# FiLM moved to tokens on partitions in both layers of a two-layer conditioned transformer block: a DMA transposes its output, ScalarE and GpSimd share the normalizations, ScalarE masks V

## The chip, the cores and the metric

The kernel runs on one core of one Trainium2 chip. The metric is device time in microseconds of one execution; the lower the better. The number to beat is the median of three runs of the kernel before, 825.99 us (822.73 to 827.06).

## The reference, cut to what matters

Two layers run one after the other on `x` of shape (32, 256, 256): 32 independent batches of 256 tokens with 256 features. Layer 0 is linear attention with 8 heads (softmax of Q over a head's 32 features, of K over the tokens), layer 1 is full attention with 16 heads of 16 features. Both end in the same way, and the change is about this ending and about the layer norms.

```python
# layer 0 (x: b, t, d)
xn = ln(x) * ln_w + ln_b
q = softmax(heads(xn @ Wq + bq), axis=-1)
k = softmax(heads(xn @ Wk + bk + (1 - mask) * -1e6), axis=tokens)
v = heads((xn @ Wv + bv) * mask)
y = q @ (k.T @ v)
# layer 1
xn = ln(x) * norm_w + norm_b
att = softmax(q @ k.T + (1 - mask) * -1e6, axis=keys)
v = (xn @ v_w + v_b) * mask
y = att @ v
# the ending of each layer ("FiLM")
scale, shift = split(silu(cond) @ W_emb + b_emb)          # per batch, 256 features each
h = ln(y) * ln2_w + ln2_b
h = silu(h * (1 + scale) + shift) @ W_out + b_out
x = x + h
```

So in the ending a row of `A` and a row of `B` per batch (both 256 long, made once in the setup from scale, shift, ln2_w and ln2_b) are applied to the normalized `y`, silu follows, and a matmul with `W_out`.

## The kernel before, in words

A batch is two blocks of 128 tokens on the partitions, 256 features along the free dimension ([128, 2, 256], 512 fp32 values in each partition). The kernel streams the 32 batches through some 60 small pieces; each piece is one to eight instructions on one engine, and has a semaphore that counts batches. The order of the pieces is written out by hand in one list for each engine (the lists of calls such as `rows(12, 3); cols(11, 4); ...`), so every engine works in a fixed order and waits for the semaphores of the piece that is next. Layer 0 runs several batches ahead of layer 1, so that in most of the program all engines hold work of both layers. PSUM has 8 banks; tables (`BANK`, `FREED`) say which bank a piece writes for each batch and what has to be finished before. All DMAs are issued by SyncE ("SPq" in the profile), also from one written list.

Pieces that the change touches, each with a suffix 0 or 1 for the layer:

- Norm of x (`a`, `n`, `r`, `c`, `h`, `z`): VectorE aggregates mean and variance (L1207), ScalarE writes minus the mean (`nm`, L1681) and variance plus epsilon (`ve`, L1682), GpSimd takes the power -1/2 (`rs`, L2011), GpSimd writes the normalized `Z` (two instructions of 256, L2015), GpSimd rounds it to fp16 (`h`, L2029), GpSimd subtracts for the remainder (`z`, L2036). The fp16 pair `ZHL` is transposed by a DMA (L531) and feeds the matmuls; each projection is three fp16 products (high x high, low x high, high x low), 12 matmuls in all.
- Norm of y (`yn`, L2015 with `YN`), by GpSimd, with tokens on partitions.
- FiLM: TensorE transposes `YN` (`y0T`, `y1T`: four 128x128 fp32 transposes in a bank, L723). With features on partitions, `A` and `B` of a batch are one number in each partition, so ScalarE applies them as scale and bias of an activation straight from PSUM: `TH` = tanh(h/2) (L1758) and `HH` = h (L1761), two instructions of 256 each. VectorE makes `ST` = (TH + 1) * HH (L1278). ScalarE rounds it to fp16 (`SH`, L1771), GpSimd subtracts for the remainder (L2088), and the output projection reads the pair (L708 with `wo`).
- Mask of V in layer 1 (`vm`, L2129): GpSimd, two instructions of 256.

The other large consumers are the scores of layer 1, computed twice: as rows (L835, with VectorE's maximum L1308 behind it, 8 pieces of four matmuls in a batch) and as columns (L848, with ScalarE's exponential L1807 behind it), then the product with V (L861).

Of the kernel before, what the change touches and what calls it, by code (L numbers as in the profile page):

```python
# [29 lines left out]
    "gpm": "1",  # L30
    "gt_w0": "0",
    "grow3": "2",
    "ga_w0": "0",
    "gt_o0": "3",
    "gcnd": "4",
    "gbb0": "5",
    "ga_o0": "3",
    "gbb1": "0",
    "gk0": "24753705446136211562401264736663",
    "gq0": "42207151427077545476112375444722",  # L40
    "gfx0": "6",
    "gv0": "75642771253063150447530557625531",
    "gkt": "66726405663127011101160224236724",
    "gfm0": "3",
    "gat": "65212575415247151554334140721664",
    "gqt": "73355127624732065226236537346625",
    "gt_f0": "3",
    "gy0": "25750625603626114224256013761365",
    "ga_f0": "4",
    "gy0T": "42355207464664435223011576172432",  # L50
    "gt_w1": "1",
    "ga_w1": "1",
    "go0": "05413576502340043030735727070451",
    "grw": "6",
    "gcol": "6",
    "gt_b": "4",
    "gt_o1": "0",
    "ga_b": "4",
    "gfx1": "1",
    "gq1": "44704575141572521727150770612041",  # L60
    "ga_o1": "0",
    "gk1": "75525464633014417236046551205400",
    "gfm1": "3",
    "gt_f1": "4",
    "gbb2": "2",
    "gv1": "64057773630271362144236527064014",
    "gr0": "00402404646460424404200042262666",
    "gr1": "62206262662206620026644420602242",
    "gr2": "20622202222220660020444444260466",
    "gr3": "62624600022200624246404264020442",  # L70
    "gr4": "02664642426266600642200260006626",
    "gr5": "26022200042600006026040424264222",
    "gr6": "62204402044006044042460246206600",
    "gr7": "26640640022262066220206664662262",
    "ga_f1": "6",
    "gc0": "66426404266406666262424400644262",
    "gc1": "20002246622242422000020042264004",
    "gc2": "60042246260062646020604422046660",
    "gc3": "62422004646244460644620060624202",
    "gc4": "46206646662204044604426046062024",  # L80
    "gpv0": "14062153063330626002061215650456",
    "gc5": "66404004646604464266226402462060",
    "gpv1": "15143460474541250413602344706447",
    "gpv2": "45043560446454250516700255304554",
    "gc6": "20606626000222626620064660624002",
    "gc7": "00224244662606662264242026460020",
    "gty0": "46056577455433510066701742216543",
    "gpv3": "31754730007352047562301275105572",
    "gty1": "33267244665003044624440055105472",
    "gy1T": "71477300023554175724706543174653",  # L90
    "go1": "77002057550012516235333440150322",
# [189 lines left out]
def up(n):  # L281
    return max(n, 0)


def bass_cond_seq(
# [7 lines left out]
    with ctx:  # L293
# [407 lines left out]
        def _(e):  # L701
# [318 lines left out]
            def fm0():  # L1020
                film(0)
# [1244 lines left out]
```

## Time and profile before

| | before |
|---|---|
| median of 3 runs | 825.99 us |
| the profiled execution | 826.59 us |
| its span (first to last instruction) | 824.9 us |
| PE busy | 797.7 us (97%) |
| DVE busy | 735.6 us (89%) |
| ACT busy | 704.5 us (85%) |
| POOL busy | 688.7 us (83%) |
| granted TensorE clock | 0.989 |

PE is TensorE, PEld its weight loads (they run beside the matmuls), DVE is VectorE, ACT ScalarE, POOL GpSimd, SPq the queue of SyncE that issues DMAs. Busy is the time in which at least one instruction of the engine runs. Instructions of one engine overlap at their ends: the next one starts before the last has ended. So what an instruction costs in an engine that is never idle is the distance from its start to the next start, which is less than its duration. A timeline row merges neighbours of one kind: start, length of the merged stretch, what, and how many.

### The profile page before, as it was taken

How to read it: one execution, taken by the hardware profiler on the slowest of the kernel's cores; microseconds unless marked ns; L12 is line 12 of the kernel's file. 1: busy time of each engine (PE TensorE's matmuls, PEld its weight loads, DVE VectorE, ACT ScalarE, POOL GpSimd, SP SyncE). 2: the span in 40 equal slices, each digit the busy share in tenths (PEclk: the TensorE clock that was granted, in tenths of full speed). 3: DMA queues.
4: the chain of work that ended last, by engine and by line, in shares of the span. 5: the costliest groups of instructions: out<-in, count | busy, mean ns of one | idle time of the engine just before them, and what ended most of it. 6: DMA issues, size and time to landing. Idle time of an engine off the chain costs nothing.

```text
span 824.9 us, 27262 instructions
## 1 busy us (share of the span) xinstructions
PE 797.7 (97%) x9407; PEld 572.0 (69%) x9407; DVE 735.6 (89%) x1488; ACT 704.5 (85%) x1658; POOL 688.7 (83%) x1021
## 2 busy tenths in 40 slices
PE   7998999999999999999999999999999999999995
PEld 3575776777777777677777777777777777666643
DVE  6899999998989999989898889989898989898962
ACT  2366678999898998898898998889989999999995
POOL 8579899999878999789898999888889987896423
PEclk9899999999999999999999999999999999999998
DMA  7522355354344443334545543353454433444411
GB/s 184 153 40 67 96 140 133 81 119 112 86 108 109 105 126 102 98 90 98 122 107 136 121 98 84 84 134 106 110 122 109 109 88 80 99 104 128 116 34 39
DMA packets 149276, 86.11 MB, mean 104 GB/s; under 512 B 87404, under 2 KB 141802, under 8 KB 149130
## 3 DMA queue, kind: packets, MB, share of 16 engines
q1 hardware_dynamic: 149140, 84.36, 42.4%
q8 instruction: 77, 1.26, 0.7%
q14 instruction: 59, 0.48, 0.2%
HBM read 39.64 MB, written 25.80 MB: 79 GB/s over the span
## 4 chain that ended last, share of the span: by engine, by line
PE 41%; issue 12%; POOL 9%; DVE 9%; DMA 2%; SPq 1%; ACT 1%; POOLq 0%; DVEq 0%; ACTq 0%
PE banks L708 11%; PE banks L861 7%; PE banks L716 5%; PE banks L835 4%; PE banks L848 4%; PE banks L723 3%; DVE NM L1308 3%; PE banks L738 2%; PE banks L787 2%; PE banks L871 2%; DVE st L1199 1%; POOL YN L2015 1%; POOL rs L2011 1%; POOL ZHL L2036 1%; POOL SH L2088 1%
## 5 line engine op out<-in xcount | busy, mean ns | idle before, releaser
L1308 DVE TENSOR_REDUCE NM<-banks 128x4 f32<-128x1024 f32 x256 | 306.4, 1212 | 25.1 <-PE banks L835 24.0
L1807 ACT ACTIVATE wraw<-banks 128x1024 f32<-128x1024 f32 x154 | 155.9, 1034 | 8.0 <-PE banks L848 7.3
L2011 POOL TENSOR_TENSOR rs<-ve,nhalf 128x2 f32<-128x2 f32 x128 | 89.7, 703 | 31.6 <-ACT ve L1682 31.4
L1807 ACT ACTIVATE PX<-banks 128x1024 f32<-128x1024 f32 x102 | 103.5, 1035 | 8.6 <-PE banks L848 7.3
L2088 POOL TENSOR_TENSOR SH<-ST,SH 128x512 f16<-128x512 f32 x64 | 74.4, 1164 | 31.4 <-ACT SH L1771 31.4
L708 PE MATMUL banks<-wo,SH 128*128 128x256 f16 x768 | 94.9, 274 | 4.5 <-POOL SH L2088 4.4
L708 PE MATMUL banks<-wv,ZT 128*128 128x256 f16 x768 | 93.5, 273 | 1.4 <-DVE wv L1404 0.5
L835 PE MATMUL banks<-SK,SQ 51*128 51x256 f16 x1024 | 92.5, 272 | 0.8 <-ACT wemb L1815 0.3
L848 PE MATMUL banks<-SQ,SK 53*128 53x256 f16 x1024 | 90.6, 271 | 2.1 <-DVE NM L1308 1.0
L2036 POOL TENSOR_TENSOR ZHL<-Z,ZHL 128x256 f16<-128x256 f32 x128 | 87.5, 704 | 2.6
L861 PE MATMUL banks<-wraw,V 128*32 128x256 f32 x1232 | 87.2, 385 | 0.8 <-DVE NM L1308 0.8
L708 PEld LDWEIGHTS banks<-wo,SH 128*128 128x128 f16 x768 | 72.1, 98 | 20.7 <-POOL SH L2088 7.1
L708 PEld LDWEIGHTS banks<-wv,ZT 128*128 128x128 f16 x768 | 73.0, 98 | 15.3 <-issue 7.3
L2115 POOL TENSOR_TENSOR AB<-R,AB 128x512 f16<-128x512 f32 x64 | 74.6, 1168 | 3.8 <-ACT AB L1787 3.5
L2015 POOL TENSOR_SCALAR Z<-X,nm,rs 128x256 f32<-128x256 f32 x128 | 73.9, 586 | 4.2 <-issue 2.5
L1787 ACT ACTIVATE R<-banks,fcs 128x256 f32<-128x256 f32 x128 | 62.3, 487 | 12.3 <-PE banks L716 12.0
L1758 ACT ACTIVATE TH<-banks,hB,hA 128x256 f32<-128x256 f32 x128 | 65.8, 571 | 7.6 <-PE banks L723 6.9
L2015 POOL TENSOR_SCALAR YN<-Y,nm,rs 128x256 f32<-128x256 f32 x128 | 70.1, 557 | 1.3
L848 PEld LDWEIGHTS banks<-SQ,SK 53*128 53x128 f16 x1024 | 39.9, 94 | 41.7 <-issue 24.0
L1761 ACT ACTIVATE HH<-banks,fB,fA 128x256 f32<-128x256 f32 x128 | 66.2, 581 | 0.0
L835 PEld LDWEIGHTS banks<-SK,SQ 51*128 51x128 f16 x1024 | 38.8, 94 | 36.8 <-issue 23.0
L1787 ACT ACTIVATE AB<-banks,fcs 128x256 f16<-128x256 f32 x128 | 62.8, 491 | 0.0
(186 smaller groups left out, 1879.5 us busy)
## 6 DMA issues: line engine op xcount, KB each, us to landing
scr<-AB SPq DMA_DIRECT2D x64, 256.0 KB, 2.6
X<-in_x_dram SPq DMA_DIRECT2D x32, 256.0 KB, 2.8
SK<-scr SPq DMA_DIRECT2D x64, 128.0 KB, 2.9
SQ<-scr SPq DMA_DIRECT2D x64, 128.0 KB, 2.7
out_dram<-wemb SPq DMA_DIRECT2D x32, 256.0 KB, 2.5
SK<-scr SPq DMA_DIRECT2D x64, 64.0 KB, 2.9
SQ<-scr SPq DMA_DIRECT2D x64, 64.0 KB, 2.7
wemb<-in_L_cond_W_emb_dram SPq DMA_DIRECT2D x1, 1024.0 KB, 5.5
```

What stands on the lines that cost most here:

```text
L708: m = PE.matmul(dst[:, t, :], zt[:, j, k, t * P:(t + 1) * P], w[:, i, k, :], start=(k, n) == (0, 0), stop=(k, n) == (1, 2))
L835: m = PE.matmul(banks[:, n + j % 2, (j // 2) * T:(j // 2) * T + T], SQ[p, r, h, c * P:(c + 1) * P], SK[p, r, h, :], start=True, stop=True)
L848: m = PE.matmul(banks[:, n + j % 2, (j // 2) * T:(j // 2) * T + T], SK[p, r, h, c * P:(c + 1) * P], SQ[p, r, h, :], start=True, stop=True)
L861: m = PE.matmul(banks[32 * j:32 * j + 32, n, 0:T], V1[:, r, c, 4 * g + j, :], px((8 * b + u) % 5)[:, at_px(j):at_px(j) + T], start=(c == 0 ...
L1308: V.tensor_reduce(NMe[:, c, :, 2 * g:2 * g + 2], banks[:, n:n + 2, :].rearrange("p a (h m) -> p a h m", m=T), AX.X, ALU.max, negate=True). ...
L1787: t = A.activation(dst, bank(home(f"g{c}1", b))[:, f, :], ACT.Identity, bias=fcs[:, i, f:f + 1], scale=(r_q, r_k)[i])
L1807: A.activation(px(v % 5), banks[:, n:n + 2, :].rearrange("p a n -> p (a n)"), ACT.Exp, scale=r_uu).then_inc(S["exp"])
L2011: G.tensor_tensor(rs[:, b % 2, l, :], ve[:, b % 2, l, :], nhalf[:, :], ALU.pow).then_inc(S[f"r{l}"])
L2015: i = G.tensor_scalar(dst[:, t, :], src[:, t, :], nm[:, b % 2, l, t:t + 1], rs[:, b % 2, l, t:t + 1], ALU.add, ALU.mult)
L2036: i = G.tensor_tensor(ZHL[:, l, b % 2, 1, k], z[:, :, k, :], ZHL[:, l, b % 2, 0, k], ALU.subtract)
L2088: G.tensor_tensor(SH[:, l, 1], ST[:, l], SH[:, l, 0], ALU.subtract).then_inc(S[f"sl{l}"])
L2115: G.tensor_tensor(AB[:, i, :, 1], R1[:, i], AB[:, i, :, 0], ALU.subtract).then_inc(S["sp" + c])
```

## The change

FiLM is done with tokens on partitions. The row `A` and the row `B` of a batch (`FR`, [128, 2, 256]) are spread to all partitions by a DMA for each batch and layer (`fr0`, `fr1`) from a table in DRAM that is written once (`fw0`, `fw1`). The normalized y goes straight to `HH`; GpSimd multiplies it by `A` (`fa`) and adds `B` (`fb`), 512 wide each; ScalarE takes the tanh of `HH`, in one instruction of 512 from SBUF (`th`); `ST` is as before; `SHL` is its fp16 pair with the remainder in two halves; a DMA transposes it (`sT0`, `sT1`, [128, 1024] fp16) into `SHT`, which the output projection reads. TensorE's transposes `y0T` and `y1T`, and their banks, are gone.

Three smaller parts: the rounding to fp16 in the norms of x (`h0`, `h1`), the normalized x of layer 0 (`c0`), the normalized y of layer 0 (`yn0`) and the mask of V (`vm`) go from GpSimd to ScalarE; where ScalarE normalizes, VectorE makes -mean*rs first (`m0`, `my0`); where GpSimd does (`c1`, `yn1`), it subtracts the mean that VectorE aggregated, so that ScalarE's `nm` is gone. In the setup, VectorE prepares the rows with batches on 32 partitions (`film_token`). All lists of order and the bank tables are written anew.

```diff
             def o0(b):
-                e.wait_ge(S["sl0"], b + 1)
+                e.wait_ge(d_s[0][b % 2], 16 * (b // 2 + 1))
...
-            def y0T(b):
-                e.wait_ge(S["yn0"], b + 1)
-                clear(e, "gy0T", b)
-                transposes(home("gy0T", b), YN[:, 0]).then_inc(S["y0T"])
...
+            def film_in(b, l, i):
+                e.wait_ge(S[f"fb{l}"], b)
+                if b == 0:
+                    e.wait_ge(l_fm[l], 16)
+                e.dma_start(FR[:, i].rearrange("p a n -> p (a n)"), fmd[l, b].unsqueeze(0).to_broadcast([P, 2 * D])).then_inc(d_fr[l][b % 2], 16)
+
+            def turn_out(b, l, i):
+                e.wait_ge(S[f"sl{l}"], b + 1)
+                e.wait_ge(S[f"o{l}"], b)
+                e.dma_start(SHT[:, i].rearrange("p j k (t n) -> p (j k t) n", t=2),
+                            SHL[:, i].rearrange("p j k t n -> p (j k t n)"), transpose=True).then_inc(d_s[l][b % 2], 16)
...
+            def m0(b):
+                e.wait_ge(S["r0"], b + 1)
+                e.wait_ge(S["c0"], up(b - 1))
+                for t in range(2):
+                    i = V.tensor_scalar(nmr[:, b % 2, 0, t:t + 1], mv[:, b % 2, 0, t, 0:1], rs[:, b % 2, 0, t:t + 1], -1.0,
+                                        ALU.mult, ALU.mult)
+                i.then_inc(S["m0"])
...
-                A.activation(nm[:, b % 2, l, :], mv[:, b % 2, l, :, 0], ACT.Copy, scale=-1.0)
...
-                for k in range(2):
-                    A.activation(TH[:, l, k, :], bank(n)[:, k, :], ACT.Tanh, bias=hB[:, l, k, b:b + 1],
-                                 scale=hA[:, l, k, b:b + 1])
-                for k in range(2):
-                    i = A.activation(HH[:, l, k, :], bank(n)[:, k, :], ACT.Identity, bias=fB[:, l, k, b:b + 1],
-                                     scale=fA[:, l, k, b:b + 1])
+                e.wait_ge(S["fb0"], b + 1)
+                e.wait_ge(S["st0"], b)
+                A.activation(TH[:, 0], HH[:, 0], ACT.Tanh, scale=r_t[0]).then_inc(S["th0"])
...
+            def h0(b):
+                e.wait_ge(S["c0"], b + 1)
+                if b >= 2:
+                    e.wait_ge(d_z[0][b % 2], 16 * (b // 2))
+                A.activation(ZHL[:, 0, b % 2, 0].rearrange("p k t n -> p t k n"),
+                             Z[:, 0].rearrange("p t (k n) -> p t k n", k=2), ACT.Identity).then_inc(S["h0"])
...
+            def c0(b):
+                e.wait_ge(S["m0"], b + 1)
+                e.wait_ge(S["z0"], b)
+                for t in range(2):
+                    i = A.activation(Z[:, 0, t, :], X[:, b % 3][:, t, :], ACT.Identity, bias=nmr[:, b % 2, 0, t:t + 1],
+                                     scale=rs[:, b % 2, 0, t:t + 1])
+                i.then_inc(S["c0"])
...
+            def fa0(b):
+                e.wait_ge(S["yn0"], b + 1)
+                e.wait_ge(d_fr[0][b % 2], 16 * (b // 2 + 1))
+                G.tensor_tensor(HH[:, 0], HH[:, 0], both(FR[:, 0, 0, :]), ALU.mult).then_inc(S["fa0"])
+
+            def fb0(b):
+                e.wait_ge(S["fa0"], b + 1)
+                G.tensor_tensor(HH[:, 0], HH[:, 0], both(FR[:, 0, 1, :]), ALU.add).then_inc(S["fb0"])
```

What the change does to ScalarE's order is shown at one place in the middle of the program. Before, from the start of `th1` of some batch (`banks` is PSUM, `wemb` here the buffer of the transposed attention output, `PX` and `wraw` the buffers of exponentials):

```order
L1807 ACTIVATE PX<-banks 128x1024
L1815 ACTIVATE wemb<-banks 128x256
L1807 ACTIVATE wraw<-banks 128x1024
L1758 ACTIVATE TH<-banks,hB,hA 128x256 x2
L1761 ACTIVATE HH<-banks,fB,fA 128x256 x2
L1736 ACTIVATE AT<-banks 32x2x32 x4
```

ScalarE after, near the same place, with `yn0` (L1933), `c0` (L1925), `h0` (L1911) and `th0` (L1788):

```order
L1933 ACTIVATE HH<-Y,nmr,rs 128x256 x2
L1828 ACTIVATE wraw<-banks 128x1024
L1730 ACTIVATE KE,ks<-banks,km 128x256 x2
L1708 ACTIVATE ve<-mv,epa 128x2
L1925 ACTIVATE Z<-X,nmr,rs 128x256 x2
L1911 ACTIVATE ZHL<-Z 128x2x2x128
L1788 ACTIVATE TH<-HH 128x512
L1753 ACTIVATE QT<-banks,rk 128x256 x2
```

The four instructions of FiLM from PSUM became one from SBUF, and `h0` stands straight behind the `c0` whose result it reads.

SyncE's queue, also in the middle. Before, the DMA transposes there are of `ZT` (layer inputs) and `NT` (row maxima):

```order
L588 DMA_TRANSPOSE NT<-NMw 128x2x128
L524 DMA X<-in_x_dram 128x2x256
L595 DMA ntd<-NT 32x256
L531 DMA_TRANSPOSE ZT<-ZHL 128x8x128
L551 DMA scr<-AB 128x4x256
L602 DMA SQ<-ntd 2x2048 x2
```

SyncE after, with the transposes of FiLM's output (L522) and the rows `FR` (L517):

```order
L522 DMA_TRANSPOSE SHT<-SHL 128x8x128
L560 DMA_TRANSPOSE ZT<-ZHL 128x8x128
L617 DMA_TRANSPOSE NT<-NMw 128x2x128
L522 DMA_TRANSPOSE SHT<-SHL 128x8x128
L573 DMA augm<-mbd 3x256
L517 DMA FR<-fmd 128x512
L624 DMA ntd<-NT 32x256
```

In each batch two transposes and two spreading DMAs are new, and `ZT` and `NT` stand among them in one queue.

## Rows read from the trace of the kernel before

**Rows 1.** The page's first part: busy time of each engine over the span.
```profile
PE 797.7 (97%) x9407; PEld 572.0 (69%) x9407; DVE 735.6 (89%) x1488; ACT 704.5 (85%) x1658; POOL 688.7 (83%) x1021
```
**Rows 2.** Windows of the span: each engine's busy time, clock, DMA share.
```profile
0.00:100.00 100.00, 89.58 (x735) 60.96 (x737) 88.17 (x249) 52.90 (x157) 78.75 (x129) 0.93 0.45 106
100.00:700.00 600.00, 594.34 (x7327) 441.82 (x7330) 550.41 (x1074) 541.15 (x1289) 536.22 (x789) 1.00 0.45 108
700.00:800.00 100.00, 98.80 (x1204) 61.50 (x1198) 88.76 (x148) 95.34 (x187) 65.48 (x95) 1.00 0.38 99
800.00:825.00 25.00, 14.97 (x152) 7.72 (x148) 8.23 (x21) 15.14 (x29) 8.23 (x10) 0.91 0.13 43
```
**Rows 3.** The same window for L1308 alone, eight in a batch.
```profile
100.00:700.00 600.00, 246.73 (x207) 1.00 0.45 108
```
**Rows 4.** Timeline of PE at 407 us: two neighbouring groups of four transposes.
```profile
407.67 0.60 PE L723 MATMUL banks<-ident,KE 128*128 128x128 f32 x4
408.10 0.60 PE L723 MATMUL banks<-ident,QE 128*128 128x128 f32 x4
```
**Rows 5.** Timeline of ACT from 399 us: start, stretch, what.
```profile
399.45 0.68 ACT L1720 ACTIVATE QE<-QS 128x512 f32<-128x512 f32 x1
399.97 0.25 ACT L1681 ACTIVATE nm<-mv 128x2 f32<-128x2 f32 x1
400.06 0.34 ACT L1682 ACTIVATE ve<-mv,epa 128x2 f32<-128x2 f32 x1
...
403.54 0.47 ACT L1704 ACTIVATE KE<-banks,km 128x256 f32<-128x256 f32 x1
403.90 0.20 ACT L1704 ACTIVATION_READ_ACCUMULATOR KE<-banks,km 128x1 f32 x1
...
418.91 1.02 ACT L1758 ACTIVATE TH<-banks,hB,hA 128x256 f32<-128x256 f32 x2
419.82 1.02 ACT L1761 ACTIVATE HH<-banks,fB,fA 128x256 f32<-128x256 f32 x2
```
**Rows 6.** Timeline of POOL from 419 us: `c0` and `vm`.
```profile
419.63 1.10 POOL L2015 TENSOR_SCALAR Z<-X,nm,rs 128x256 f32<-128x256 f32 x2
...
429.02 0.93 POOL L2129 TENSOR_SCALAR V<-V1t,mcol 128x256 f32<-128x256 f32 x2
```
**Rows 7.** Groups of POOL's lines: busy us, mean ns of one | idle before.
```profile
L2036 POOL TENSOR_TENSOR ZHL<-Z,ZHL 128x256 f16<-128x256 f32 x128 | 87.5, 704 | 2.6
L2088 POOL TENSOR_TENSOR SH<-ST,SH 128x512 f16<-128x512 f32 x64 | 74.4, 1164 | 31.4 <-ACT SH L1771 31.4
L2029 POOL TENSOR_SCALAR ZHL<-Z 128x256 f16<-128x256 f32 x128 | 54.5, 441 | 2.9
L2071 POOL TENSOR_TENSOR XB<-X,bobc 128x512 f32<-128x512 f32 x32 | 40.7, 1273 | 4.6 <-DVE X L1289 4.5
```
**Rows 8.** Timeline of DVE at 410 us: a pair of tiny instructions, the next one.
```profile
410.79 0.25 DVE L1207 BATCH_NORM_AGGREGATE mv<-st 128x2 f32<-128x6 f32 x2
410.97 0.75 DVE L1289 SCALAR_TENSOR_TENSOR X<-banks,un,XB 128x512 f32<-128x512 f32 x1
```
**Rows 9.** L1278 alone: count, duration ns min/median/max.
```profile
L1278 DVE SCALAR_TENSOR_TENSOR ST<-TH,HH x64: 629/693/1678, 49.9 to 816.9; 128x512 f32<-128x512 f32 x64
```
**Rows 10.** L1278 as a group: busy us, mean ns | idle before.
```profile
L1278 DVE SCALAR_TENSOR_TENSOR ST<-TH,HH 128x512 f32<-128x512 f32 x64 | 51.9, 816 | 4.0 <-ACT HH L1761 4.0
```
**Rows 11.** L531 alone: SyncE's time for one (min/median/max ns), and its landing.
```profile
L531 SPq DMA_TRANSPOSE ZT<-ZHL x64: 1231/1241/2533, 14.5 to 762.4; - x64
...
DMA to landing us min/median/max: 3.0/3.2/5.6
```
**Rows 12.** Waits of SyncE's queue, the largest: us in total, times, longest.
```profile
SPq L588 <- DVE NMw L1313: 114.6, 28, 7.5
```
**Rows 13.** Timeline at 813 us: the last batch's `yn1` and `st1`.
```profile
813.13 1.09 POOL L2015 TENSOR_SCALAR YN<-Y,nm,rs 128x256 f32<-128x256 f32 x2
...
816.94 0.69 DVE L1278 SCALAR_TENSOR_TENSOR ST<-TH,HH 128x512 f32<-128x512 f32 x1 [3.63 <-ACT HH L1761]
```

More of the change, by code:

```diff
@@ L275 @@
 PIECES = (
-    "s0 a0 n0 r0 c0 h0 z0 xb0 k0 km kn ke ktT kt rk q0 q1 qm qs qe qtT qt qd rq v0 v att at y0 Y0 s1 a1 n1 r1 "
-    "yn0 y0T th0 st0 sh0 sl0 o0 x1 s2 a2 n2 r2 c1 h1 z1 xb1 q1p qa spq k1p ka spk v1p vt vm rows max nh np cols "
-    "exp pv yt ty rd Y1 s3 a3 n3 r3 yn1 y1T th1 st1 sh1 sl1 o1 o").split()
+    "s0 a0 n0 r0 m0 c0 h0 z0 xb0 k0 km kn ke ktT kt rk q0 q1 qm qs qe qtT qt qd rq v0 v att at y0 Y0 s1 a1 n1 r1 "
+    "my0 yn0 fa0 fb0 th0 st0 sh0 sl0 o0 x1 s2 a2 n2 r2 c1 h1 z1 xb1 q1p qa spq k1p ka spk v1p vt vm rows max nh np cols "
+    "exp pv yt ty rd Y1 s3 a3 n3 r3 yn1 fa1 fb1 th1 st1 sh1 sl1 o1 o").split()
 def up(n):
@@ L408, in bass_cond_seq @@
         ST = sb("ST", [P, 2, 2, T])
-        SH = sb("SH", [P, 2, 2, 2, T], F16)
+        FR = sb("FR", [P, 2, 2, D])
+        SHL = sb("SHL", [P, 2, 2, 2, 2, P], F16)
+        SHT = sb("SHT", [P, 2, 2, 2, T], F16)
+        tsc = sb("tsc", [P, 2])
         AB = sb("AB", [P, 2, 2, 2, T], F16)
@@ new lines, in _ @@
+            x_in(24); wq(18); rk6(18); rq6(18); fr1(15); sT1(14); z1T(19); sT0(20); nT(17); am(26); nw(17)
+            out_(14); z0T(24); nr(17); fr1(16); x_in(25); wk(19); fr0(22); wq(19); rk6(19); rq6(19); sT1(15)
+            z1T(20); nT(18); sT0(21); out_(15); nw(18); z0T(25); x_in(26); fr0(23); fr1(17); wk(20); nr(18); wq(20)
+            rk6(20); am(27); z1T(21); rq6(20); sT1(16); nT(19); sT0(22); nw(19); nr(19); z0T(26); fr0(24); wk(21)
+            x_in(27); wq(21); rk6(21); am(28); rq6(21); sT1(17); z1T(22); fr1(18); sT0(23); nT(20); nw(20)
@@ L1204, in moments @@
                 e.wait_ge(S[f"s{l}"], b + 1)
-                e.wait_ge(S[f"n{l}"], up(b - 1))
+                e.wait_ge(S[("c0", "yn0", "c1", "yn1")[l]], up(b - 1))
                 for t in range(2):
@@ L1674, in _, with spread @@
             r_un, r_q, r_k, r_uu = (e.alloc_register(n) for n in ("r_un", "r_q", "r_k", "r_uu"))
-            def mean_of(b, l):
+            r_t = [e.alloc_register(f"r_t{l}") for l in range(2)]
+            def spread(b, l):
                 k, a = l % 2, (ZS ** -2, 1.0)[l % 2]
@@ L2137, in yn1, with fa1, fb1 @@
                 e.wait_ge(S["r3"], b + 1)
-                e.wait_ge(S["y1T"], b)
-                apply(b, 3, YN[:, 1], Y[:, 1], "yn1")
-            def sl1(b):
-                sl_of(b, 1)
+                e.wait_ge(S["st1"], b)
+                apply(b, 3, HH[:, 1], Y[:, 1], "yn1")
+            def fa1(b):
+                e.wait_ge(S["yn1"], b + 1)
+                e.wait_ge(d_fr[1][b % 2], 16 * (b // 2 + 1))
+                G.tensor_tensor(HH[:, 1], HH[:, 1], both(FR[:, 1, 0, :]), ALU.mult).then_inc(S["fa1"])
+            def fb1(b):
+                e.wait_ge(S["fa1"], b + 1)
+                G.tensor_tensor(HH[:, 1], HH[:, 1], both(FR[:, 1, 1, :]), ALU.add).then_inc(S["fb1"])
+            def sl1(b):
+                e.wait_ge(S["sh1"], b + 1)
+                for k in range(2):
+                    i = G.tensor_tensor(SHL[:, 1, 1, k], ST[:, 1].rearrange("p t (k n) -> p t k n", k=2)[:, :, k, :],
+                                        SHL[:, 1, 0, k], ALU.subtract)
+                i.then_inc(S["sl1"])
             def cst():
```

1283 lines of the change are left out of this document (647 added, 636 removed), and 178 rows, old and new, of the table FREED.

## The prediction, made before the changed kernel was run

> **What bounds the kernel now.** I read the busy times of the page first [rows 1]: TensorE is at 97% and the others at 83 to 89%. The windows say where the missing 27 us of TensorE are [rows 2]: 10.4 in the first 100 us (setup and the first batches), 5.7 in the 600 us between 100 and 700, 1.2 in the next 100, 9.9 in the last 25. So from 100 to 800 us TensorE is the bound: it works 99% of the time at the full clock (1.00, the 2.4 GHz level), while VectorE idles 50 us of the 600, ScalarE 59, GpSimd 64. Those idle times are waits on a saturated TensorE and on each other, and they are the slack that an edit of these engines can use. The window of L1308 shows 207 of eight in a batch [rows 3], so the 600 us hold about 25.8 batches, 23.3 us each; TensorE's share of that is 23.0.
>
> **What an instruction costs.** With engines this full the distance of starts counts, not the duration. Four fp32 transposes take 0.43 us from start to start [rows 4]. On ScalarE, 512 values from SBUF without operands in SBUF take 0.52 (399.45 to 399.97), a tiny one 0.09, 256 values from PSUM with one operand per partition 0.36, with two 0.455 (two in 0.91) [rows 5].
>
> **The change part by part, per batch.**
>
> TensorE loses two groups of four transposes. 0.43 each where they stand beside their like; groups that begin behind a wait cost a little more, so I take 0.45: -0.90 us, 23.3 over the middle's 25.8 batches and 29 over 32. The output projections stay 12 matmuls. The setup loses eight small transposes, under 1 us.
>
> ScalarE loses eight activations of 256 from PSUM with two operands (8 x 0.455 = 3.64) and four `nm` (0.36): -4.0. It gains two `th` and two `h` of 512 from SBUF (4 x 0.52 = 2.08), four of 256 with two operands for `c0` and `yn0`, and two with one for `vm` (0.72). `c0` and `yn0` read SBUF with two operands per partition, for which the trace has no row; the nearest rows are 0.36 and 0.52, and I take the two-operand row, 0.455: 1.82. Sum +4.62, net +0.62. In its order `h0` stands straight behind the `c0` that it reads, which loses the overlap of neighbours, about 0.1. I take +0.7: ScalarE's 541 us of the middle become 559. (The Trainium skill, "ScalarE: Activation LUTs", section "What ACT_TABLE_LOAD costs", gives for an activation 186 ns + 0.833 per value, 93 per pointer operand, and an overlap of 93: an estimate of 0.49 for `c0`, and 0.14 more per batch than the row. The two-operand row at 0.455 is below that.)
>
> GpSimd loses `h` (4 x 0.41), `c0` (1.10), `yn0` (1.08 by the same line) and `vm` (0.93) [rows 6, 7], and the 512-wide remainder of `SH`, twice 1.14: together -7.0. It gains four remainders of 256 (the row of its like: 87.5/128 = 0.68, 2.73) and `fa`, `fb` twice: 512 fp32 values with a row repeated over the tokens, of which `XB` is the exact form: 1.27 less the overlap of 0.03, 4 x 1.24 = 4.96. Net +0.7: 536 become 554.
>
> VectorE gains four tiny `m0`, `my0`. Two tiny instructions take 0.18 between starts [rows 8], so 0.09 each: +0.36; 550 become 560. The upper bound is the whole stretch of a pair, 0.25, for each pair plus a wait for GpSimd's `rs` in front; that would be +1.
>
> SyncE's queue gains two transposes at 1.24 us and two `FR` DMAs at 0.4 (an estimate from its other DMAs in the timeline), +3.3 us of issuing per batch. Its DMAs issue for 377 us in all now, so this becomes 483. The data: 64 x 256 KB spread and 64 transposes more, on a DMA share of 0.45 [rows 2]; I expect about 0.6 and landings still near 3.2 us [rows 11]. These latencies are hidden in the middle, since layer 0 and layer 1 each have 23 us per batch and the buffers `HH`, `SHL`, `SHT`, `FR` are held for 5 to 10 of them.
>
> One thing speaks against moving work onto fp32 GpSimd instructions with two inputs. `ST` on VectorE has both inputs in SBUF, a median of 0.69 us but a mean of 0.82 and a maximum of 1.68 [rows 9, 10]: 8 us over 64 are lost to something in the way. The Trainium skill, "SBUF — State Buffer", section "Who interferes with whom", says that a VectorE instruction with two SBUF inputs and a GpSimd instruction that reads SBUF lock each other out for the whole instruction. By that rule the loss follows the number of long GpSimd instructions (over 1 us), which goes from 7 to 9 per batch: about 2 us more. Without the rule the term is zero; the sum does not need it.
>
> **The sum.** The work of the middle becomes TensorE 571, VectorE 560, ScalarE 559, GpSimd 554, where it was 594, 550, 541, 536. TensorE still has most, but if nothing else idled the others would have 2 to 3% of slack instead of 8 to 11. The middle can't get shorter than 577 (571 and the old 5.7 of idle); at 600 nothing is gained. At 577 the waits of VectorE would have to fall from 50 to 17 and of ScalarE from 59 to 18. I take it that they halve, since half of them are only the echo of a full TensorE: VectorE 585, ScalarE 588, GpSimd 586. So 586, -14 us. From 700 to 800 TensorE saves about seven groups (3 us); ScalarE is at 95% there and gains a little on layer 1's share; -2. The first 100 us: TensorE's saving there is 2 to 3 us, but the first output of layer 0 now waits for two GpSimd passes and a transpose; -1. The end: from the last `yn1` to the last `st1` were 3.8 us [rows 13]; now 1.1 + 2.5 (`fa`, `fb`) + 0.6 (`th`) and three handoffs, about 4.4; behind `sl1`, which is 0.2 longer, comes a transpose that lands in 3.2: +4. Sum: -14 - 2 - 1 + 4 = -13, of 826.6 us (span 824.9 and 1.7 around it; the median of the runs is 0.6 below): 813.6. I forecast 814.
>
> **The rivals.**
>
> Full gain: the waits of the other engines are all echoes, and the middle falls to 577. Then -23 - 3 - 2 + 4 = -24: 802. For it: TensorE's 5.7 us of idle in 600, which shows how well a written order keeps one engine full. Against it: no second engine was within 8% of it there.
>
> Nothing left: four engines at 93 to 95% each trip over one another, and the waits of ScalarE and VectorE hardly shrink. With 50 of VectorE's waits kept, the middle is 610, with 40 it is 600. At 600 the time is 826.6 - 1 - 1 + 4 = 828. For it: every saved TensorE microsecond comes with more handoffs (`rs` by GpSimd, `nmr` by VectorE, `c0` by ScalarE were two engines' work).
>
> Slower: SyncE's queue becomes the bound. It works in order, and its waits add to 390 us (14 rows, the largest 115 for the row maxima [rows 12]), issuing to 377: it had nearly 60 us left for nothing. Now 483 us go to issuing, and `sT0`, `sT1` wait for GpSimd's remainder and stand in front of `ZT` and `NT` transposes whose results TensorE needs. Each time that one of these is late by more than its lead, TensorE waits about one landing, 3.2 us. Four such events eat the gain; from there on it is slower. With eight in 32 batches: 814 + 26 = 840. Against it: TensorE waited for DMAs under 3 us in the whole run, so the leads are long. Price and place are SyncE's queue between `sT` and `z0T`, `nT`, `z1T`.
>
> **How the numbers follow.** Forecast as worked out, with its own range 806 to 821: 0.53. Full gain: 0.10. Nothing left, 822 to 831: 0.17. Slower, 831 to 855: 0.20. The range 802 to 838 leaves out about 2 in 10. Half a percent of 826 is 4.1 us, about what a measurement of this kernel can tell from no change: faster is below 821.9, slower above 830.1. Faster 0.63, same 0.15, slower 0.22.
>
> **What would show it.** In the profile after: TensorE busy near 769 us and no group of `YN`; ScalarE near 725, GpSimd near 710, VectorE near 747. `fa` and `fb` at a mean of 1.27 us; `th` at 0.64; `c0`, `yn0` on ScalarE at 0.57. TensorE's idle from 100 to 700 us at about 15 us per 585, and VectorE's and ScalarE's each halved. The step is wrong if TensorE's idle in the middle stays at 6 us (full gain) or grows to 25 (nothing left). The slower rival shows as TensorE or its weight loads waiting for DMA `ZT`, `SHT` or `SQ` for tens of us. The forecast would also be wrong if ScalarE's instructions from SBUF with two operands were much above 0.6, or if the two GpSimd passes ran longer than `XB` does.

## The result

| | before | after |
|---|---|---|
| median | 826.52 us (4 runs) | 913.29 us (4 runs, 908.26 to 915.57) |
| ratio to before | 1 | 1.1049 [1.0989, 1.1108] |
| span of the profiled execution | 824.9 us | 913.9 us |
| granted TensorE clock | 0.989 | 0.964 |

The changed kernel is 87 us slower. The forecast was 814, with a range up to 838: it is wrong in sign and far outside. None of the four cases described the main cost. Medians here are of all runs, while ratios and their 95% intervals leave out the few runs in which the chip was in its slower state, so a difference of two medians and the same difference by ratios can be a few us apart.

### The profile page after: what moved, and what is told of

Same layout as the page of the kernel before. It is cut to its first block and busy times, and to the rows that moved or that the text cites. A ratio compares the mean times of both kernels' runs of the same rounds, so it can differ in the third digit from the quotient of the medians.

```text
span 913.9 us, 26896 instructions
## 1 busy us (share of the span) xinstructions
PE 797.4 (87%) x9143; PEld 549.6 (60%) x9143; DVE 762.9 (83%) x1606; ACT 730.4 (80%) x1592; POOL 792.7 (87%) x893
## 5 line engine op out<-in xcount | busy, mean ns | idle before, releaser
L2086 POOL TENSOR_TENSOR rs<-ve,nhalf 128x2 f32<-128x2 f32 x128 | 94.3, 738 | 39.1 <-ACT ve L1708 38.7
L884 PE MATMUL banks<-SQ,SK 53*128 53x256 f16 x1024 | 94.4, 274 | 25.5 <-ACT wraw L1828 6.9
L749 PE MATMUL banks<-wo,SHT 128*128 128x256 f16 x768 | 96.7, 277 | 22.9 <-DMA SHT<-SHL 22.3
L871 PE MATMUL banks<-SK,SQ 51*128 51x256 f16 x1024 | 94.5, 275 | 11.8 <-DMA SQ<-scr 3.7
L749 PE MATMUL banks<-wv,ZT 128*128 128x256 f16 x768 | 97.0, 278 | 3.0 <-ACT wemb L1836 1.4
L749 PEld LDWEIGHTS banks<-wo,SHT 128*128 128x128 f16 x768 | 72.9, 99 | 40.9 <-DMA SHT<-SHL 27.0
L749 PEld LDWEIGHTS banks<-wv,ZT 128*128 128x128 f16 x768 | 73.9, 99 | 19.9 <-issue 10.4
L2090 POOL TENSOR_SCALAR HH<-Y,mv,rs 128x256 f32<-128x256 f32 x64 | 80.2, 1259 | 2.5
L2090 POOL TENSOR_SCALAR Z<-X,mv,rs 128x256 f32<-128x256 f32 x64 | 80.2, 1262 | 2.1
L1305 DVE SCALAR_TENSOR_TENSOR ST<-TH,HH 128x512 f32<-128x512 f32 x64 | 55.8, 871 | 16.2 <-ACT TH L1848 16.1
L1210 DVE BATCH_NORM_STATS2 st<-X 128x6 f32<-128x256 f32 x128 | 47.5, 413 | 19.7 <-DMA X<-in_x_dram 19.3
L1708 ACT ACTIVATE ve<-mv,epa 128x2 f32<-128x2 f32 x128 | 37.1, 295 | 30.4 <-DVE mv L1218 30.1
```

The lines of the kernel that those rows point to most:

```text
L749: m = PE.matmul(dst[:, t, :], zt[:, j, k, t * P:(t + 1) * P], w[:, i, k, :], start=(k, n) == (0, 0), stop=(k, n) == (1, 2))
L871: m = PE.matmul(banks[:, n + j % 2, (j // 2) * T:(j // 2) * T + T], SQ[p, r, h, c * P:(c + 1) * P], SK[p, r, h, :], start=True, stop=True)
L884: m = PE.matmul(banks[:, n + j % 2, (j // 2) * T:(j // 2) * T + T], SK[p, r, h, c * P:(c + 1) * P], SQ[p, r, h, :], start=True, stop=True)
L1305: V.scalar_tensor_tensor(out=ST[:, l], in0=TH[:, l], scalar=1.0, in1=HH[:, l], op0=ALU.add, op1=ALU.mult).then_inc(S[f"st{l}"])
L2086: G.tensor_tensor(rs[:, b % 2, l, :], ve[:, b % 2, l, :], nhalf[:, :], ALU.pow).then_inc(S[f"r{l}"])
L2090: i = G.tensor_scalar(dst[:, t, :], src[:, t, :], mv[:, b % 2, l, t, 0:1], rs[:, b % 2, l, t:t + 1], ALU.subtract, ALU.mult)
```

## The profile after

First the page's busy times, to be read against [rows 1].

```profile
PE 797.4 (87%) x9143; PEld 549.6 (60%) x9143; DVE 762.9 (83%) x1606; ACT 730.4 (80%) x1592; POOL 792.7 (87%) x893
```

ScalarE (730, forecast 725) is near what the prediction said. GpSimd was to be at 710 and is at 792.7. TensorE was to be at 769 and is at 797.4. The windows of the kernel after, in the columns of [rows 2] (stretch, length, busy time of PE, PEld, DVE, ACT, POOL, then clock, DMA share, GB/s), say where that matters:

```profile
0.00:100.00 100.00, 85.22 (x648) 53.65 (x649) 78.93 (x248) 54.47 (x142) 64.60 (x92) 0.88 0.50 122
100.00:700.00 600.00, 538.74 (x6498) 387.16 (x6495) 527.40 (x1080) 519.30 (x1147) 561.04 (x624) 0.99 0.61 138
700.00:800.00 100.00, 89.42 (x1076) 63.11 (x1074) 87.84 (x169) 84.88 (x181) 93.90 (x104) 1.00 0.64 141
```

TensorE now idles 61 us of the middle's 600 where it idled 6; GpSimd, with 39 idle, is the fullest engine, from 100 to 800 us. Its groups (busy us, mean ns of one | idle before) name the lines:

```profile
L2090 POOL TENSOR_SCALAR HH<-Y,mv,rs 128x256 f32<-128x256 f32 x64 | 80.2, 1259 | 2.5
L2090 POOL TENSOR_SCALAR Z<-X,mv,rs 128x256 f32<-128x256 f32 x64 | 80.2, 1262 | 2.1
...
L2144 POOL TENSOR_TENSOR HH<-HH,FR 128x512 f32<-128x512 f32 x32 | 41.7, 1305 | 4.8 <-ACT HH L1933 3.2 <-DMA FR<-fmd 1.4
```

L2090 are `c1` and `yn1`, the normalizations that stayed on GpSimd. In its timeline of after, a pair takes 2.43 us; a pair of the same shape took 1.10 in [rows 6]:

```profile
509.53 2.43 POOL L2090 TENSOR_SCALAR Z<-X,mv,rs 128x256 f32<-128x256 f32 x2
511.99 0.63 ACT L1918 ACTIVATE ZHL<-Z 128x512 f16<-128x512 f32 x1 [1.43 <-POOL Z L2090]
...
520.43 1.27 POOL L2148 TENSOR_TENSOR HH<-HH,FR 128x512 f32<-128x512 f32 x1
```

The shape, the types and the number of operands are as before. What differs is the form: (x - mean) * rs, `subtract` and `mult`, in place of (x + (-mean)) * rs. The second row shows the handoff that becomes late: ScalarE idled 1.43 us for that `Z`. Added up, ScalarE waited 35 us for it and 20 us in `th1` for the end of `fb1` (us in all, times, longest), while `rs` still waits for ScalarE's `ve`:

```profile
ACT ZHL L1918 <- POOL Z L2090: 35.2, 25, 2.6
ACT TH L1848 <- POOL HH L2199: 19.7, 18, 6.0
PEld banks L749 <- DMA SHT<-SHL: 27.0, 17, 8.9
PE banks L749 <- DMA SHT<-SHL: 22.3, 12, 8.6
POOL rs L2086 <- ACT ve L1708: 38.7, 33, 8.6
```

The two rows before the last are a second finding: TensorE waits 22 us for the new transposes `SHT` (L749 is the output projection). These events are few and long. Only 9.1 of the 22.3 us, in 8 events of up to 2.2 us, lie between 100 and 700 us; 12.2 us, in 3 events, come after 700, at the end of the program.

## The experiments

Twelve kernels ran. The base of most is the first one, "nm and add". All but the third, which ran once, have a ratio to before with its 95% interval. The kernel before ran beside each series (medians 825.3 to 826.8), so kernels of different series are best compared by their ratios.

**1. nm and add: the changed kernel with the old form of the normalization.**

```diff
+                if l >= 2:
+                    A.activation(nm[:, b % 2, l, :], mv[:, b % 2, l, :, 0], ACT.Copy, scale=-1.0)
...
-    i = G.tensor_scalar(dst[:, t, :], src[:, t, :], mv[:, b % 2, l, t, 0:1], rs[:, b % 2, l, t:t + 1],
-                        ALU.subtract, ALU.mult)
+    i = G.tensor_scalar(dst[:, t, :], src[:, t, :], nm[:, b % 2, l, t:t + 1], rs[:, b % 2, l, t:t + 1],
+                        ALU.add, ALU.mult)
```

> The changed kernel with one part undone: in layer 1's two norms ScalarE again writes minus the mean (a tiny activation) and GpSimd adds it, instead of subtracting the mean that VectorE aggregated. Theory S (GpSimd's instruction with subtract costs double, 1.26 against 0.57 us, and GpSimd is the bound): L2090's group falls to 0.56 to 0.60 us, GpSimd's busy time falls by 84 us to about 709, and the time falls by most of that, to 812 to 830. Rival Q (SyncE's queue and the landings of the new transposes bound it; GpSimd's length is beside the point): GpSimd's busy falls, but TensorE's wait for SHT stays at 22 us and more and the time stays above 885. Rival L (VectorE and GpSimd lock each other out, and that made the instructions long): they stay at 1.2 us and the time stays.

Measured: 847.72 us (839.87 to 852.98), ratio 1.023 [1.0193, 1.0268]. Of the 87 us, 66 are gone (68 by the ratios), although ScalarE got 64 instructions more. The page, GpSimd's group, the pair in its timeline and the middle of this kernel:

```profile
PE 780.9 (92%) x9143; PEld 545.2 (64%) x9143; DVE 756.2 (89%) x1606; ACT 731.4 (86%) x1656; POOL 712.5 (84%) x893
```
```profile
L2093 POOL TENSOR_SCALAR Z<-X,nm,rs 128x256 f32<-128x256 f32 x64 | 38.2, 606 | 2.1
```
```profile
505.74 1.10 POOL L2093 TENSOR_SCALAR Z<-X,nm,rs 128x256 f32<-128x256 f32 x2
```
```profile
100.00:700.00 600.00, 570.38 (x7038) 416.97 (x7037) 563.23 (x1164) 558.82 (x1282) 546.50 (x675) 0.99 0.65 150
```

GpSimd's 712.5 is the 710 of the forecast, so the price of every other GpSimd instruction was right. But the time is 34 us above the forecast and 18 above the upper end of what this experiment expected, and TensorE idles 30 us of the middle: something else remains.

**2. The kernel before with subtract.** Only the normalizations of layer 1.

```diff
-  ... ACT.Copy, scale=-1.0)
+  ... ACT.Copy, scale=-1.0 if l < 2 else 1.0)
-  ... rs[:, b % 2, l, t:t + 1], ALU.add, ALU.mult)
+  ... rs[:, b % 2, l, t:t + 1], ALU.add if l < 2 else ALU.subtract, ALU.mult)
```

> The kernel before with one edit: in layer 1's two norms (128 of the 256 instructions) ScalarE writes plus the mean and GpSimd subtracts it. The operands lie where they lay. Theory S: those instructions take 1.2 us instead of 0.56, GpSimd's busy time rises by 84 us to 772, and since it had 64 us of slack per 600 in the middle, most of 84 lands: 870 to 905. Rival P (the aggregated mean, an operand that VectorE wrote two values apart, is what is slow to read): nothing changes, 826, and the instructions stay at 0.56. Rival Q: nothing changes either.

Measured: 885.22 us, ratio 1.0722 [1.0699, 1.0744]. GpSimd's busy time goes from 688.7 to 777.6:

```profile
PE 809.9 (92%) x9407; PEld 573.5 (65%) x9407; DVE 741.4 (84%) x1488; ACT 707.4 (80%) x1658; POOL 777.6 (88%) x1021
```

```profile
L2015 POOL TENSOR_SCALAR Z<-X,nm,rs 128x256 f32<-128x256 f32 x128 | 117.4, 927 | 4.2 <-issue 2.5 <-POOL ZHL L2037 0.2
L2015 POOL TENSOR_SCALAR YN<-Y,nm,rs 128x256 f32<-128x256 f32 x128 | 113.2, 895 | 1.3
```

In each of these two groups half of the instructions have the subtract. Together they were at 144.0 us in the kernel before and are at 230.6: 86.6 us over 128 instructions, 0.68 each. The operands are the tiles of before; only the operation (and the sign of a tile) changed. So it is the operation that costs it, in the kernel before too, and not FiLM or the aggregated mean as an operand. About two thirds of GpSimd's added time reached the end (59 of 89 us).

**3. Which form.** After, with `c1` as (add `mv`, mult `rs`) and `yn1` as (mult `rs`, subtract `mv`). These two values are then not the norm.

```diff
+                    if l == 2:
+                        i = G.tensor_scalar(..., mv[:, b % 2, l, t, 0:1], rs[:, b % 2, l, t:t + 1], ALU.add, ALU.mult)
+                    else:
+                        i = G.tensor_scalar(..., rs[:, b % 2, l, t:t + 1], mv[:, b % 2, l, t, 0:1], ALU.mult, ALU.subtract)
```

> The changed kernel with another arithmetic in layer 1's norms, so what it computes there is not the norm: c1 adds the aggregated mean and multiplies (add, mult, the mean read where VectorE wrote it), yn1 multiplies by rs first and subtracts the mean second (mult, subtract). Theory S with subtract slow in either place: Z<-X at 0.56 to 0.60 us, HH<-Y at 1.2. If only a subtract in the first place is slow: both at 0.6. Rival P (the operand's place): both at 1.2. Time if only one of the two is long: about 42 us of GpSimd's 84 come back, 860 to 885.

Measured once: 884.35 us, and

```profile
L2094 POOL TENSOR_SCALAR HH<-Y,rs,mv 128x256 f32<-128x256 f32 x64 | 79.4, 1247 | 2.5
...
L2091 POOL TENSOR_SCALAR Z<-X,mv,rs 128x256 f32<-128x256 f32 x64 | 37.6, 596 | 2.1
```

Reading the mean from the strided `mv` is free (596 with add); a subtraction in the second place costs as much as in the first (1247). GpSimd's busy time fell by 40 us and the time by 29. That settles the first cause.

**4 to 7. Who holds "nm and add"?** Four edits of it, each taking one load away. No spread: the rows `FR` are spread for batch 0 only, so later batches use row 0. GpSimd relief: `fb` adds `B` to 2 of 512 columns. VectorE relief: two of eight row maxima over half the keys. ScalarE relief: `th` and the rounding `h` over half of their columns. The cuts show the main line of each edit; the comments behind `#` are added here.

```diff
+                if b:
+                    return          # film_in (no spread)
```
```diff
-  G.tensor_tensor(HH[:, 0], HH[:, 0], both(FR[:, 0, 1, :]), ALU.add)
+  G.tensor_tensor(HH[:, 0, 0, 0:2], HH[:, 0, 0, 0:2], FR[:, 0, 1, 0:2], ALU.add)     # GpSimd relief
```
```diff
+                w = T // 2 if u % 4 == 1 else T                    # VectorE relief: max_ over [..., 0:w]
```
```diff
-  A.activation(TH[:, 0], HH[:, 0], ACT.Tanh, ...)
+  A.activation(TH[:, 0, 0:2 if b == 0 else 1], HH[:, 0, 0:2 if b == 0 else 1], ACT.Tanh, ...)   # ScalarE relief
```

> The changed kernel with the norms of layer 1 added as before (e1, 848 us), and the rows A and B spread to all partitions for batch 0 alone, so later batches use batch 0's rows: 62 DMAs of 256 KB fewer, 16 MB. Theory D (what e1 still has over the forecast comes from DMA traffic and SyncE's queue: TensorE waits 21 us for SHT): the DMA share in the middle falls from 0.65 to about 0.5, SHT waits shrink, and the time falls by 10 us or more, to 838 or less. Rival E (the engines, each at 91 to 95 percent of the middle, hold one another up): within 4 us of e1.

> e1 with fb, GpSimd's addition of B, done for 2 of its 512 columns: GpSimd has 74 us less work, 2.3 per batch, and the chain from yn to the output is 1.2 us shorter. Theory E with GpSimd as a holder: 10 to 25 us faster than e1, 823 to 838. Theory D or another engine as the holder: within 5 us of e1, most of the rest by the shorter end of the program.

> e1 with two of the eight row maxima of a batch taken over half of the keys: VectorE has 34 us less work, 1.07 per batch. Theory E with VectorE (94 percent busy in the middle, the most after TensorE) as the holder: 10 to 25 us faster than e1, 823 to 838. Otherwise within 4 us of it.

> e1 with th and h on half of their columns from the second or third batch on: ScalarE has 27 us less work, 0.86 per batch. Theory E with ScalarE (93 percent busy in the middle) as the holder: 8 to 20 us faster than e1, 828 to 840. Otherwise within 4 us of it.

| | median us | ratio to before | against "nm and add", by medians (by ratios) |
|---|---|---|---|
| no spread | 836.83 | 1.0125 [1.008, 1.017] | -11 (-9) |
| GpSimd relief (712 to 642 us busy) | 834.0 | 1.0097 [1.006, 1.0133] | -14 (-11) |
| VectorE relief (756 to 727) | 843.39 | 1.0214 [1.015, 1.0277] | -4 (-1) |
| ScalarE relief (731 to 710) | 848.48 | 1.0245 [1.0184, 1.0306] | +1 (+1) |

"nm and add" itself is known only within some 3 us, so each difference is good to about 5. Relief of VectorE or of ScalarE alone gives nothing that can be told from none. Relief of GpSimd by 70 us, which also makes the chain from `yn` to the output shorter, returns 11 to 14, so it isn't GpSimd alone either. The DMAs of the rows, which my sum had at nothing, cost 9 to 11. Without them TensorE's wait for `SHT` between 100 and 700 us falls from 10.6 us in 9 events to 2.2 in 4. The other 10 us of the 21.0 in all are the last two projections of the program, and they stay.

**8. No transposes: `SHL` is transposed for batch 0 only.** The later projections read the old `SHT` and wait for their own batch's remainder, so they have the wrong input and the same work.

```diff
             def turn_out(b, l, i):
+                if b:
+                    return
...
             def o0(b):
-                e.wait_ge(d_s[0][b % 2], 16 * (b // 2 + 1))
+                if b == 0:
+                    e.wait_ge(d_s[0][0], 16)
+                e.wait_ge(S["sl0"], b + 1)
```

> The version with nm and add (847.7 us), but the DMA transposes of SHL into SHT are made for batch 0 only; the output projections of the later batches read the old SHT as soon as the remainder of their own batch is done (their result is wrong, their work is the same). Gone are 62 transposes: some 77 us of issuing in SyncE's queue at 1.24 each, their traffic, and a landing of 3.2 us between GpSimd's remainder and the projection. Theory one, SyncE's queue and late transposes take the middle's gain (my rival 'slower' of the forecast): TensorE's 21 us of waiting for SHT go, and about as much of the time: 826 to 830. Theory two, GpSimd's longer chain and fuller time take it, and TensorE then waits for the remainder itself: 3 us from the end of the program and 2 to 5 from the middle, 840 to 843.

Measured: 835.9 us, ratio 1.0129 [1.0089, 1.0168], -12 (-8 by ratios): between the two theories.

**9. Neither transposes nor spread** (both edits together):

> Neither transposes of SHL nor spread rows after batch 0: all of the DMAs that the change adds are gone, while all work of the five engines is as in the version with nm and add. Theory one (DMAs: queue, landings, traffic): the middle gets what the forecast gave it, 848 - 34 = 814 and 3 less at the end: 811 to 818. Theory two (the engines' own work and handoffs; TensorE's relief finds no taker): not under 826, about 830.

Measured: 828.07 us, ratio 1.0037 [1.0018, 1.0056], -20 (-16 by ratios, give or take 4). The page and the middle of this kernel:

```profile
PE 776.5 (94%) x9143; PEld 545.7 (66%) x9143; DVE 756.3 (92%) x1606; ACT 730.9 (88%) x1656; POOL 712.5 (86%) x893
```
```profile
100.00:700.00 600.00, 580.95 (x7197) 426.87 (x7194) 577.27 (x1189) 571.62 (x1310) 559.29 (x691) 1.00 0.45 110
```

With all engine work of "nm and add" and the DMA share of before (0.45), the kernel is at the time of before, not below it. So the added DMAs cost 16 to 20 us. The total is the one that the second theory gave (about 830), but its reason, that TensorE's relief finds no taker, doesn't fit the trace. In the middle VectorE idles 23 us and ScalarE 28, where they idled 50 and 59 in [rows 2]. The last addition of layer 1, one in each batch, shows where the time went (the last two times are the start of the first one and of the last one):

```profile
L1342 DVE SCALAR_TENSOR_TENSOR wemb<-banks,un,XB x32: 660/742/753, 170.2 to 821.5; 128x512 f32<-128x512 f32 x32
L1370 DVE SCALAR_TENSOR_TENSOR wemb<-banks,un,XB x32: 651/741/752, 181.8 to 842.5; 128x512 f32<-128x512 f32 x32
L1376 DVE SCALAR_TENSOR_TENSOR wemb<-banks,un,XB x32: 650/740/752, 180.6 to 822.9; 128x512 f32<-128x512 f32 x32
```

The rows are of before, of "nm and add" and of this kernel. The first output comes 10.4 us later than before, and the 31 batches behind it take 642.3 us where they took 651.3. With the end taken off at the last `yn1`, that is 632 in place of 643: 11 us faster. So the stream does gain without the added DMAs, and the start loses it again. The start is lost in the setup, before the first `FR` is fetched (at 41.6). TensorE's first projection began at 22.83 before and begins at 31.41 here (32.0 in "nm and add"), behind the matmuls that make the rows of FiLM (L1042) and of the biases, which the new order of the setup puts in front of it:

```profile
22.83 1.44 PE L738 MATMUL banks<-ZT,wk 128*128 128x256 f16 x6 [0.66 <-DVE wk L1404]
```
```profile
26.52 4.96 PE L1042 MATMUL banks<-wemb,csT 128*32 128x512 f32 x8
31.41 0.83 PE L782 MATMUL banks<-ZT,wk 128*128 128x256 f16 x6
```

No experiment put the setup back, so that these 9 us would return in full is not shown.

**10. No spread and GpSimd relief together.**

> Both reliefs at once: rows FR spread for batch 0 only, and fb over 2 of 512 columns (only these get their B). Alone they gave 11 and 14 us of 848. If they are two costs that add, 823. If both only shorten the same chain (a row of FR waits for fb of the batch before, and fa waits for the row), they give together little more than one alone: 831 to 834. With the spread gone, GpSimd relieved by 70 us and TensorE relieved by 17, a time above 826 would say that the other engines hold the kernel at its old time whatever GpSimd does.

Measured: 822.09 us, ratio 0.9966 [0.9945, 0.9987]. The two reliefs add up (26 of 25 us by medians, 22 of 20 by ratios): they are two costs and not one chain.

**11. TensorE's relief alone, on the kernel before.** The output projections leave out one of three fp16 products. By the diff it is the high part of `SH` by the low part of the weights (`PARTS` is (0, 0), (1, 0), (0, 1), weights first), and not the one that the expectation names; the number of matmuls is the same for both.

```diff
                         for n, (i, j) in enumerate(PARTS):
+                            if few and n == 1:       # few: only for wo
+                                continue
```

> The kernel before, with the output projections of both layers over two of their three fp16 products (8 matmuls in place of 12; the product of the low part of SH with the high part of the weights is left out). That is TensorE's relief alone: 8 x 0.107 = 0.86 us per batch, 27 in all, where the change takes 0.90. All other engines, orders and DMAs are as before. The forecast's step (other engines' waits halve when TensorE is relieved): -12 or -13, 813 to 815. Full gain: 801. Nothing left (the engines at 90 to 92% hold each other at the old time): 823 to 827.

Measured: 823.25 us, ratio 0.9964 [0.9945, 0.9982], -3. The expectation put the relief at 27 us of TensorE. Its page shows less, 18.7 (797.7 to 779.0), so the step as forecast would give -9.

```profile
PE 779.0 (95%) x9151; PEld 545.6 (66%) x9151; DVE 736.0 (90%) x1488; ACT 703.2 (86%) x1658; POOL 687.9 (84%) x1021
```
```profile
100.00:700.00 600.00, 582.72 (x7191) 423.54 (x7188) 554.04 (x1076) 542.49 (x1294) 538.00 (x793) 1.00 0.45 108
```

TensorE idles 17.3 us of the middle instead of 5.7, and the others' idle times hardly change (VectorE 46 for 50, ScalarE 58 for 59, GpSimd 62 for 64). That is what the rival "nothing left" described, in a kernel where nothing else was touched.

**12. All engines relieved, on the kernel before.** The last edit, and besides ScalarE leaves out one of two tanh instructions per layer, GpSimd makes half of the remainder of `SH`, VectorE takes two of eight maxima over half the keys.

```diff
-                for k in range(2):
+                for k in range(2 if b == 0 else 1):
                     A.activation(TH[:, l, k, :], bank(n)[:, k, :], ACT.Tanh, bias=hB[:, l, k, b:b + 1],
...
-                G.tensor_tensor(SH[:, l, 1], ST[:, l], SH[:, l, 0], ALU.subtract)
+                w = 2 if b == 0 else 1
+                G.tensor_tensor(SH[:, l, 1, 0:w], ST[:, l, 0:w], SH[:, l, 0, 0:w], ALU.subtract)
```

> The kernel before with the output projections of 8 matmuls, as in the last run (823.3 us), and in addition each other engine relieved by about 0.9 us per batch: ScalarE leaves out one of two tanh instructions of each layer (after batch 0), GpSimd makes the remainder of SH for half of its columns, VectorE takes two of eight row maxima over half the keys. Left out are thus parts of these three results. Theory 'all engines hold each other' (the other engines at 90 to 92% with their handoffs are as near to the bound as TensorE): now all can follow, and the middle shortens by what each loses, some 0.7 us per batch: 826 - 18 to 23 = 803 to 808. Theory 'something else holds it' (a chain through a semaphore that no engine's work shortens, or SyncE's queue): as in the last run, 818 to 824.

Measured: 810.31 us, ratio 0.9823 [0.9787, 0.9859], -15.

```profile
PE 775.0 (96%) x9151; PEld 548.5 (68%) x9151; DVE 701.9 (87%) x1488; ACT 677.8 (84%) x1596; POOL 657.4 (81%) x1021
```

Relieving the three others by 25 to 34 us each brings 12 us on top of the 3, and TensorE's busy share is back at 96%. This is a little short of the 18 to 23 expected of the theory that the engines hold each other, and well outside the 818 to 824 of its rival. It doesn't say which of the three counted most.

No kernel that does all of the work beat the one before.

## Why the prediction was wrong

**The step that failed first: the price of `c1` and `yn1`.** The part on GpSimd counts what it loses and gains, and says nothing of the two normalizations that stay, which leaves them at the price of [rows 6]. The diff changed them from add to subtract, the text of the change says so ("it subtracts the mean that VectorE aggregated"), and I counted only the `nm` that this saves on ScalarE. It costs 4 x 0.66 = 2.6 us per batch on GpSimd, whose busy time is 792.7 instead of 712.5. Shown by experiments 1, 2 and 3; worth 66 to 68 of the 87 us. The guard at the end of the prediction looked at `fa` and `fb` and at ScalarE's new forms, not at this one.

**The second: the first 100 us, taken at -1.** The term weighed TensorE's saving against a later first output, but not the new order of the setup, in which the first projection begins 9 us later. The first output of layer 1 came 10 to 12 us later than before (170.2 to 180.6 in experiment 9, 181.8 in "nm and add").

**The third: "These latencies are hidden in the middle".** The added DMAs cost 16 to 20 us (experiment 9), 9 to 11 by the spreads alone (4), 8 to 12 by the transposes alone (8). In the two traces "nm and add" loses 15.7 us to experiment 9 from the first output to the last `yn1`, and 2.7 in the end behind it. The traffic came out as forecast (share 0.61 to 0.65 for 0.6, `SHT` landing in 3.2). But TensorE waited 21 us for `SHT` in "nm and add", 10.6 of it between 100 and 700 us in events of up to 3.3, the rest at the last two projections:

```profile
PE banks L750 <- DMA SHT<-SHL: 21.0, 11, 7.5
```

The rival "Slower" had waits of TensorE for `ZT`, `SHT` or `SQ` as its sign, and its 831 to 855 holds the 848 of "nm and add". For the kernel as it was changed it was nearest, though still 58 us short. How much of the 16 to 20 is issuing in SyncE's queue, how much traffic and how much the landing itself stays open: each edit removed the three together.

**The middle: "I take it that they halve".** The sum took 14 us from 100 to 700 us and 2 behind on the grounds that half of the other engines' waits were echoes of a full TensorE. With the added DMAs gone (experiment 9) VectorE's and ScalarE's waits did halve, and from the first output to the last `yn1` 11 of these 16 us came, although TensorE's busy time had fallen by 21 us and not by 29 (797.7 to 776.5). But the grounds aren't shown: experiment 11 takes 18.7 us from TensorE alone, all else as before, and gets 3 in place of 9. What else in the changed kernel made its middle faster stays open. So the rival "nothing left" came near the total of experiment 9 (828) by luck, with a gain in the middle and a loss at the start that it didn't have. For relief of TensorE alone it was right.

**What was right.** `fa` and `fb` took 1.27 to 1.35 us (1.27), `th` 0.63 (0.64), ScalarE's busy time is 730 (725). The tail: in "nm and add", from the last `yn1` to the last `st1`, 829.66 to 834.13 = 4.5 us (4.4), then the landing, and from `yn1` to the end 16.2 us where it was 11.8: +4.4 (+4). Partly this is luck: 0.9 us of it is the last projection at a lower clock (2.74 us for 1.86), which the sum didn't have.

```profile
829.66 1.09 POOL L2093 TENSOR_SCALAR HH<-Y,nm,rs 128x256 f32<-128x256 f32 x2
...
834.13 0.69 DVE L1306 SCALAR_TENSOR_TENSOR ST<-TH,HH 128x512 f32<-128x512 f32 x1 [5.15 <-ACT TH L1851]
...
836.89 1.23 SPq L523 DMA_TRANSPOSE SHT<-SHL  x1
839.70 2.26 PEld L750 LDWEIGHTS banks<-wo,SHT 128*128 128x128 f16 x12 [7.75 <-DMA SHT<-SHL]
839.71 2.74 PE L750 MATMUL banks<-wo,SHT 128*128 128x256 f16 x12 [7.47 <-DMA SHT<-SHL]
```

**Small misses.** ScalarE's two-operand instructions from SBUF took 0.49 from start to start where I took 0.455. Their mean is 0.60 (0.57):

```profile
L1928 ACT ACTIVATE Z<-X,nmr,rs 128x256 f32<-128x256 f32 x64 | 35.0, 599 | 4.3 <-DVE nmr L1242 4.1
```

So the estimate of 0.49, worked out from the figures of the Trainium skill ("ScalarE: Activation LUTs", "What ACT_TABLE_LOAD costs"), was the better number than the row from PSUM. VectorE's `m0` and `my0` are busy for 20.4 us in "nm and add", 0.16 for each of 128 instructions, where I took 0.09. This is why VectorE is at 756 and not at 747. `ST` went from a mean of 816 ns [rows 10] to 838 in "nm and add" and 871 in the kernel after, 1.7 and 3.9 us over 64. The prediction had about 2 for this, by the number of long GpSimd instructions. The direction fits, but no run isolates it.

**The whole.** Three rows of "last addition of layer 1" are above; with the others they give (us from the start of the program; the profiled execution of each):

| | first output | last output | between |
|---|---|---|---|
| before | 170.2 | 821.5 | 651.3 |
| after | 190.3 | 910.5 | 720.2 |
| nm and add | 181.8 | 842.5 | 660.7 |
| 9: no added DMAs | 180.6 | 822.9 | 642.3 |
| 11: TensorE relieved | 169.1 | 817.4 | 648.3 |
| 12: all relieved | 168.4 | 805.1 | 636.7 |

Before 826; +10 at the start, -11 in the stream, +2 at the end (experiment 9, 828); the added DMAs +16 to 20 (848); the subtraction +66 to 68 (913).

## What to carry to other kernels

Price every instruction whose operation changes as a new instruction, also where shape, operands and engine stay: on GpSimd an fp32 subtraction of a scalar took twice the time of an addition of its negative. Where one engine is at 97% and three are at 83 to 89%, relief of the first alone was worth little here (3 us for 19), and relief of all about half of what each lost (15 us for 23 to 34). DMAs that are added to a stream can cost time in the middle too: here 16 to 20 us for 124 of them, with an engine in a fixed order waiting for some of their results (10.6 us between 100 and 700). And a total that didn't move is no proof that nothing was gained: cut it into start, stream and end before naming the cause.

## What the hardware showed unexpectedly

GpSimd's fp32 tensor_scalar on 128x256 took 596 to 606 ns (mean) with add and mult, and 1247 to 1262 with a subtract in either place. TensorE's granted clock at the end of the program: the last projection, 12 matmuls, took 2.74 us in "nm and add" after 7.47 us of idle, at a granted clock of 0.50, the 1.2 GHz level. The projection before it, after 2.92 us of idle (at 830.75 in the same timeline), took 1.48. In the kernel before, the last projection came after 2.70 us of idle and took 1.86, at 0.76. The windows are of "nm and add" and of before:

```profile
830.75 1.48 PE L750 MATMUL banks<-wo,SHT 128*128 128x256 f16 x12 [2.92 <-DMA SHT<-SHL]
```
```profile
839.70:842.50 2.80, 2.74 (x12) 1.64 (x12) 0.01 (x1) 0.00 (x0) 0.00 (x0) 0.50 0.00 0
819.50:821.50 2.00, 1.86 (x12) 1.20 (x12) 0.02 (x1) 0.00 (x0) 0.03 (x1) 0.76 0.26 86
```

This isn't the transpose's doing alone. In experiment 9, which has none there, TensorE idled 6.32 us for `fa`, `fb`, `th` and the remainder, and its last projection took 2.74 us as well:

```profile
820.16 2.74 PE L752 MATMUL banks<-wo,SHT 128*128 128x256 f16 x12 [6.32 <-POOL SHL L2215]
```

So the transpose costs the end 2.7 us (16.2 from the last `yn1` to the end, 13.5 without it), and the longer chain in front of it the 0.9 us of the lower clock.
